# A two-layer graph network and an edge attention on one core: x scaled earlier, key rows turned in two parts, stores on another queue, and a rotated order of the attention

## The reference

```
h = relu(layernorm(x));  deg = max(edges into node, 1);  norm = deg ** -0.5
twice:   h = rrelu( segment_sum((rel[type] + h[src]) @ W_r, dst) * norm + where(no edge in, h @ W_el, h @ W_sl) )
x = x + h
h = relu(layernorm(x));  qk = h @ Wqk + bqk;  v = h @ Wv + bv
score(e) = clip(qk[dst] . qk[src] / sqrt(128), -5, 5);  a = softmax of score over the edges of one dst
out = segment_sum(a * v[src], dst) @ Wo + bo;  x = x + gamma * layernorm(out + h) + beta
```

## Time and profile before

| | us |
|---|---|
| median of three runs | 803.48 (803.4 to 803.63) |
| profiled execution | 803.2 |
| its span, first to last instruction | 800.6 |
| TensorE busy | 717.5 (90%) |
| VectorE busy | 515.5 (64%) |
| ScalarE busy | 431.3 (54%) |
| GpSimd busy | 258.0 (32%) |
| mean granted clock of TensorE | 0.984 |

### The profile page before, as it was taken

How to read it: one execution, slowest core, us unless ns; L and a number is a source line. 1 busy time by engine, 2 the same in 40 slices (tenths; PEclk the granted TensorE clock), 3 DMA queues, 4 the chain that set the end, 5 groups by cost and what they waited for, 6 DMA issues and landing times.

```text
span 800.6 us, 15393 instructions
## 1 busy us (share of the span) xinstructions
PE 717.5 (90%) x5767; PEld 533.3 (67%) x5767; DVE 515.5 (64%) x931; ACT 431.3 (54%) x1085; POOL 258.0 (32%) x273
## 2 busy tenths in 40 slices
PE   5268689897999999987999999799999999999995
PEld 3157588786889999876988999444444444444455
DVE  5999999986688877341333333434665757565667
ACT  0447866664466566652111111377676767677671
POOL 7140080000000222210000000256665766666663
PEclk9999999998999999989999999999999999999997
DMA  4101100133300000102222111210000000000000
GB/s 131 45 1 34 50 2 8 52 103 64 101 9 8 8 8 8 53 20 57 64 93 74 37 36 34 85 50 0 1 15 11 14 13 14 13 13 14 3 24 19
DMA packets 39763, 27.89 MB, mean 35 GB/s; under 512 B 5311, under 2 KB 38163, under 8 KB 39686
## 3 DMA queue, kind: packets, MB, share of 16 engines
q1 hardware_dynamic: 38356, 26.02, 11.2%
q10 hardware_dynamic: 1330, 0.86, 0.4%
HBM read 13.28 MB, written 10.80 MB: 30 GB/s over the span
## 4 chain that ended last, share of the span: by engine, by line
PE 65%; DVE 9%; DMA 8%; ACT 5%; issue 5%; SPq 5%; POOL 2%; ACTq 1%; POOLq 0%; DVEq 0%
PE sums L1467 16%; PE sums L1450 15%; PE sums L998 9%; PE sums L1071 9%; PE sums L1037 6%; DMA first_columns<-counts 2%; SPq L582 2%; DVE work L835 2%; DVE work L829 2%; SPq L572 2%; ACT counts L1243 2%; DMA h_layer_one<-work 1%; PE sums L1094 1%; PE sums L1005 1%; DMA h_attention<-work 1%
## 5 line engine op out<-in xcount | busy, mean ns | idle before, releaser
L1546 POOL TENSOR_TENSOR counts<-counts,work 125x500 f32<-125x500 f32 x150 | 165.6, 1104 | 96.7 <-DVE work L1607 89.6
L1037 PE MATMUL sums<-work 125*128 125x196 f16 (+15 forms) x1220 | 154.3, 253 | 22.3 <-DVE work L835 22.1
L1607 DVE SCALAR_TENSOR_TENSOR work<-sums,counts 125x500 f32<-125x500 f32 x150 | 101.7, 678 | 108.2 <-ACT sums L1564 108.2
L1467 PE MATMUL sums<-work 125*128 125x500 f32 (+1 forms) x350 | 159.0, 544 | 7.7 <-DVE work L1607 2.9
L1450 PE MATMUL sums<-work 128*125 128x500 f32 x300 | 150.3, 583 | 0.6 <-ACT work L1301 0.6
L1559 ACT ACTIVATE sums<-sums,work 125x500 f32<-125x500 f32 (+1 forms) x157 | 102.1, 650 | 76.3 <-PE sums L1450 73.1
L829 DVE TENSOR_TENSOR work<-work,counts 125x3024 f16<-125x3024 f16 (+1 forms) x60 | 114.2, 1903 | 36.9 <-PE sums L1039 33.7
L1243 ACT CAST counts<-sums 128x364 f32 (+38 forms) x305 | 131.8, 473 | 3.1 <-issue 1.1
L1039 PE MATMUL sums<-work 125*128 125x10 f16 (+15 forms) x800 | 131.6, 194 | 0.0
L835 DVE TENSOR_TENSOR work<-work,counts 125x4200 f16<-125x4200 f16 (+15 forms) x120 | 125.3, 1084 | 0.0
L998 PE MATMUL sums<-counts 125*128 125x250 f16 (+1 forms) x975 | 121.0, 269 | 3.4 <-ACT work L1181 3.2
(11 more groups left out here) (177 smaller groups left out, 686.5 us busy)
## 6 DMA issues: line engine op xcount, KB each, us to landing
first_columns<-counts SPq DMA_DIRECT2D x5, 610.4 KB
counts<-first_columns SPq DMA_DIRECT2D x5, 610.4 KB
counts<-counts SPq DMA_DIRECT2D x5, 468.8 KB
counts<-in_x SPq DMA_DIRECT2D x5, 312.5 KB
h_nodes<-counts SPq DMA_DIRECT2D x5, 312.5 KB
work<-in_x SPq DMA_DIRECT2D x12, 125.0 KB
x_after_messages<-work SPq DMA_DIRECT2D x12, 125.0 KB
h_attention<-work SPq DMA_DIRECT2D x12, 125.0 KB
```

The costliest lines, as they stand in the source:

```text
L1037: pe.matmul(win[:, 0:c, cols], lo[:, k * 2 * LO:k * 2 * LO + 128], m[:, k, h0 * w:(h0 + c) * w].rearrange("p (h d) -> p h d", d=w), start= ...
L1467: last = pe.matmul(ps_o[c % 2][:, 0:cols(u) // n], h3[:, j + i, :], pbuf[u % PB][:, i * NP:i * NP + cols(u) // n], start=j + i == 0, stop= ...
L1546: pool.tensor_tensor(a, a, p, ALU.add).then_inc(acc_done, 1)
L1607: dve.scalar_tensor_tensor(pbuf[u % PB], ps_s[u % 4][0:NP, 0:WIDE], float(np.exp(-CLIP)), counts[0:NP, j, c * WIDE:(c + 1) * WIDE], ALU.ma ...
```

## The change

- **Turning of keys.** TensorE turns only the first 12 of 100 rows of each key array before `first_keys`; the other rows follow once the four first copies are made, and ScalarE's later copies wait for them key by key.
- **Words.** VectorE packs `words` behind the ramp copy instead of ahead of `loc`.
- **Scaling of x.** SCALED goes from 34 to 16, ROUNDS and RESTS go forward with it; the statistics come behind batch 0, the checks behind batch 1, shift and flag behind batch 4 instead of 6, the parts of the relations behind batch 11 instead of 3. The addition of EPS goes from GpSimd to VectorE. FIRST_SLOT goes from 66 to 61.
- **Stores.** The stores of chunks 2 and 3 are issued from ScalarE's queue, at the groups `agg` + 2, which are 120 and 133.
- **Loads of layer two.** Wqk, bqk and the last rows of x are loaded from SP's queue, ahead of the first x; `weigh` waits for the three weights alone, and the first qk product and the last chunk wait for the three new ones.
- **Attention.** Target group c is (c + 1) mod 6, and source block j is (j + 4) mod 24, block 24 last, so it begins with targets 4 to 7 and source 4. Two of the first three scores are issued inside the last chunk of layer two, ahead of the turn of chunk 0. The six pieces of h3 are read in that order too, and only the fifth waits for the store of the last two chunks.

```diff
@@ -117,11 +117,12 @@
 READY = (58, 82, 100, 115, 128, 140, 151, 162, 171, 180, 189, 197, 200)
-FIRST_SLOT = 66
+FIRST_SLOT = 61
 KEY_TILES = 48
+FIRST_ROWS = KEY_TILES // RT
 MOVED = 44
@@ -339,9 +340,9 @@
-    SCALED = 34
-    ROUNDS = ((40, 45, 50, 55, 60), (48, 53, 58, 63, 68))
-    RESTS = ((12, 13, 14, 16, 17), (14, 15, 16, 18, 19))
+    SCALED = 16
+    ROUNDS = ((22, 27, 32, 37, 42), (30, 35, 40, 45, 50))
+    RESTS = ((7, 8, 10, 11, 12), (9, 10, 12, 13, 14))
@@ -576,11 +577,10 @@
                     sp.dma_start(counts[0:NP, i:i + 4, 3 * D + 48 * a:3 * D + 48 * a + 48], got[:, :, a, :]).then_inc(keys_moved, 16)
-            store(2)
             for i in range(5):
                 sp.dma_start(counts[0:NP, v, 0:3 * D], counts[0:NP, v, PART_AT:PART_AT + 3 * D]).then_inc(parts_moved, 16)
-            for c in range(3, DIRECT):
+            for c in range(4, DIRECT):
                 store(c)
@@ -602,6 +602,10 @@
             sp.wait_ge(y_done, CHUNKS)
+            sp.wait_ge(norm_set, CHUNKS)
+            sp.dma_start(wqk, wqk_d).then_inc(L["last_in"], 16)
+            sp.dma_start(bqk, bqk_d.rearrange("(p o) -> p o", o=1)).then_inc(L["last_in"], 16)
+            sp.dma_start(x_last, by_block(x, LAST)).then_inc(L["last_in"], 16)
             for i, c in enumerate(ORDER2[:-1]):
@@ -615,8 +619,10 @@
             sp.wait_ge(L["summed"], CHUNKS)
-            sp.wait_ge(L["h3_out"], 16 * LAST)
+            sp.wait_ge(L["h3_out"], 16 * (LAST - 2))
             for i, (j0, j1) in enumerate(T["h3_pieces"]):
+                if j0 == 0:
+                    sp.wait_ge(L["h3_out"], 16 * LAST)
                 if j0 == LAST * LB:
@@ -665,8 +671,7 @@
             pool.wait_ge(tables_done, 1)
-            pool.wait_ge(stats_done, NB)
-            link(pool.tensor_scalar(rstd, mv[:, :, 1], EPS, None, ALU.add))
+            pool.wait_ge(stats_done, 1)
             pool.tensor_tensor(rstd, rstd, power.broadcast_to([NP, NB]), ALU.pow).then_inc(root_x, 1)
@@ -713,13 +718,6 @@
             link(dve.tensor_tensor(by_tile(tb), by_tile(starts), over(gb), ALU.add))
-            dve.wait_ge(next_in, 16)
-            link(dve.tensor_copy(after[:, 0:1], gb[:, 1:2]))
-            link(dve.tensor_copy(after[:, 1:2], nxt_i))
-            link(dve.tensor_tensor(after, after, gb, ALU.subtract))
-            link(dve.tensor_tensor(after, after, room, ALU.min))
-            link(dve.tensor_scalar(after, after, 0.0, None, ALU.max))
-            dve.scalar_tensor_tensor(words, after, 4096.0, gb, ALU.mult, ALU.add).then_inc(words_done, 1)
             link(dve.tensor_tensor(tiles(loc), tiles(dst_i), tb[:, :, None].broadcast_to([ROWS, RT, NP]), ALU.subtract))
@@ -762,6 +760,13 @@
+            dve.wait_ge(next_in, 16)
+            link(dve.tensor_copy(after[:, 0:1], gb[:, 1:2]))
+            link(dve.tensor_copy(after[:, 1:2], nxt_i))
+            link(dve.tensor_tensor(after, after, gb, ALU.subtract))
+            link(dve.tensor_tensor(after, after, room, ALU.min))
+            link(dve.tensor_scalar(after, after, 0.0, None, ALU.max))
+            dve.scalar_tensor_tensor(words, after, 4096.0, gb, ALU.mult, ALU.add).then_inc(words_done, 1)
             for k in (0, 2):
@@ -773,7 +778,9 @@
                 for j in range(NB):
-                    dve.bn_aggr(mv[:, j, :], stat[:, j, :]).then_inc(stats_done, 1)
+                    last = dve.bn_aggr(mv[:, j, :], stat[:, j, :])
+                link(last)
+                dve.tensor_scalar(rstd, mv[:, :, 1], EPS, None, ALU.add).then_inc(stats_done, 1)
@@ -842,12 +849,12 @@
                 if b == 0:
+                    statistics()
+                if b == 1:
                     checks()
-                if b == 1:
-                    statistics()
-                if b == 3:
+                if b == 11:
                     relations()
-                if b == 6:
+                if b == 4:
                     dve.wait_ge(root_x, 1)
@@ -921,7 +928,7 @@
                 if i == LAST:
-                    dve.wait_ge(L["last_in"], 16)
+                    dve.wait_ge(L["last_in"], 16 * 3)
                 else:
@@ -953,13 +960,21 @@
             pe.wait_ge(consts, 2)
+
+            def turn(k, r0, r1):
+                out = key_ps[0:NP, k, :].rearrange("p (r t) -> p r t", t=RT)
+                for t in range(RT):
+                    last = pe.matmul(out[:, r0:r1, t], key16[k][:, t * NP:(t + 1) * NP], ident_h[0:ROWS, r0:r1], start=True, stop=True)
+                return last
+
             for k in range(4):
                 pe.wait_ge(nat_done, k + 1)
-                out = key_ps[0:NP, k, :].rearrange("p (r t) -> p r t", t=RT)
-                for t in range(RT):
-                    for r0, r1 in ((0, 64), (64, ROWS)):
-                        last = pe.matmul(out[:, r0:r1, t], key16[k][:, t * NP:(t + 1) * NP], ident_h[0:ROWS, r0:r1], start=True, stop=True)
+                last = turn(k, 0, FIRST_ROWS)
                 last.then_inc(keys_turned, 1)
+            pe.wait_ge(first_keys, 4)
+            for k in range(4):
+                turn(k, FIRST_ROWS, 64)
+                turn(k, 64, ROWS).then_inc(keys_turned, 1)
@@ -1086,7 +1101,7 @@
                 if i == 0:
-                    pe.wait_ge(L["wts"], 16 * 5)
+                    pe.wait_ge(L["wts"], 16 * 3)
                 pe.wait_ge(L["turned_out"], i + 1)
@@ -1101,6 +1116,8 @@
                 pe.wait_ge(L["h3_t_out"], i + 1)
+                if i == 0:
+                    pe.wait_ge(L["last_in"], 16 * 3)
                 pe.matmul(ps_q[:, 0:w], wqk, h3_t[:, 0:w], start=True, stop=True).then_inc(L["qk"], 1)
@@ -1134,14 +1151,16 @@
                     pe.wait_ge(L["ident"], 2)
+                if i == LAST:
+                    pe.wait_ge(L["rows"], 3)
+                    A["tensor_first"](pe, 0, 2)
                 if i:
-            pe.wait_ge(L["rows"], LAST)
-            A["tensor_first"](pe)
+            A["tensor_first"](pe, 2, 3)
@@ -1160,8 +1179,8 @@
                 act.copy(*key_copy(k, 0)).then_inc(first_keys, 1)
-            act.wait_ge(first_keys, 4)
             for k in range(4):
+                act.wait_ge(keys_turned, 5 + k)
                 for piece in (1, 2, 3):
@@ -1207,9 +1226,15 @@
+
+            act_stores = {at_slot["agg", c] + 2: c for c in (2, 3)}
             act.wait_ge(words_in, 16)
             for g in range(GROUPS):
+                if g in act_stores:
+                    c = act_stores[g]
+                    act.wait_ge(y_done, c + 1)
+                    act.dma_start(h1_dram[:, c * LB * D:(c + 1) * LB * D], t1.rearrange("p b f -> p (b f)")).then_inc(h1_out, 16)
                 if g % CHUNK == 0:
@@ -1286,9 +1311,6 @@
                 act.dma_start(t, v).then_inc(L["wts"], 16)
-            act.dma_start(wqk, wqk_d).then_inc(L["wts"], 16)
-            act.dma_start(bqk, bqk_d.rearrange("(p o) -> p o", o=1)).then_inc(L["wts"], 16)
-            act.dma_start(x_last, by_block(x, LAST)).then_inc(L["last_in"], 16)
@@ -1396,6 +1418,9 @@
+    target = lambda c: (c + 1) % FULL if c < FULL else FULL
+    source = lambda c, j: (j + AB) % (FULL * AB) if c < FULL and j < FULL * AB else j
+
     units = [(c, j, 1) for c in range(FULL) for j in range(NB)] + [(FULL, j, min(AB, NB - j)) for j in range(0, NB, AB)]
@@ -1420,7 +1445,7 @@
     def rows(v, c, h, n):
-        at = c * WIDE + 2 * h * NP
+        at = target(c) * WIDE + 2 * h * NP
         return v[at:at + n * NP, :].rearrange("(b p) f -> p b f", p=NP)
@@ -1443,18 +1468,18 @@
         c, j, n = units[u]
-        if u == NB - 1:
-            pe.wait_ge(T["rows"], -(-NB // 2))
+        if u in (FULL * AB - AB, NB - 1):
+            pe.wait_ge(T["rows"], -(-NB // 2) - (u < NB - 1))
         out = ps_s[u % 4]
         if c < FULL:
-            last = pe.matmul(out[0:NP, :WIDE], qk_t[:, j * NP:(j + 1) * NP], qk_t[:, c * WIDE:(c + 1) * WIDE], start=True, stop=True)
+            last = pe.matmul(out[0:NP, :WIDE], qk_t[:, source(c, j) * NP:(source(c, j) + 1) * NP], qk_t[:, target(c) * WIDE:(target(c) + 1) * WIDE], start=True, stop=True)
         else:
-    def tensor_first(pe):
-        for u in range(AHEAD):
+    def tensor_first(pe, u0, u1):
+        for u in range(u0, u1):
             score(pe, u)
@@ -1464,7 +1489,7 @@
             for i in range(n):
-                last = pe.matmul(ps_o[c % 2][:, 0:cols(u) // n], h3[:, j + i, :], pbuf[u % PB][:, i * NP:i * NP + cols(u) // n],
+                last = pe.matmul(ps_o[c % 2][:, 0:cols(u) // n], h3[:, source(c, j + i), :], pbuf[u % PB][:, i * NP:i * NP + cols(u) // n],
                                  start=j + i == 0, stop=j + i == NB - 1)
@@ -1495,7 +1520,7 @@
                 for s, (j0, _) in zip(T["h3_in"], T["h3_pieces"]):
-                    if j == j0:
+                    if source(c, j) == j0:
                         pe.wait_ge(s, 16)
@@ -1604,7 +1629,7 @@
         if c < FULL:
```

(6 more changed lines are left out.)

## The result

| | us |
|---|---|
| before, median of 22 runs | 804.15 (801.61 to 808.76) |
| changed, median of 22 runs | 800.89 (794.65 to 808.24) |
| ratio, 95% interval | 0.9956 [0.9939, 0.9973] |
| profiled execution after | 801.75, span 800.0 |

A forecast was written before the change was run, and what follows sets the result against it. VectorE bounds 20 to 150 us, then TensorE, with waits along SP's queue to about 345. Terms +1.65 - 6.8 - 2.7 - 1.5 = -9.35 from 803.2 gave 793.85, plus 0.28: 794.1 us; 8-in-10 range 789.5 to 799.5.

The forecast's parts named there:

- The start: Kernel start: words packed later hold ScalarE's key copies, so VectorE's first batch starts 1.45 us later; EPS adds 0.2.
- Scaling from group 16: Earlier scaling of x, about even: +1.5 us of waits against -1.5 us of VectorE's waits for TensorE taken back.
- waits for h_nodes: Early chain: VectorE's moved rests come up to half a microsecond late on the h_nodes stores, +1.5 us (0 to 5).
- all of it back: Early chain: the 1.45 us that VectorE idles for TensorE is recovered whole, -1.5 us (0 to -1.5).
- The middle: Counting: stores 2 and 3 on ScalarE's queue remove the h_layer_one wait, -6.8 us (-9 to -2).
- three place loads: Middle: ScalarE's loads at groups 132, 136, 140 fall into SP's parts moves, charged 1.2 us each, 3.6 in all.
- rival D: Middle: ScalarE's store issue at group 133 is held until SP's parts moves are issued; slower, 807 us; chance 0.07.
- Rival B: Start not held and slow place loads miss the parts moves: -2.3 and -2, 790 us; chance 0.18.
- Rival C: Middle: the gain is mostly given back, each place load costing 2.3 us, 798 us; chance 0.10.
- Layer two: First weighing waits for three loads instead of five, TensorE goes on at about 374.8: -2.7 us (0 to -3.0).
- Into the attention: Layer two's end: scores ahead of the last turn and earlier h3 pieces start the first weighted sum sooner, -1.5 us.
- Rival A: Early chain costs 6 us instead of 1.65, through ScalarE's pace and the landing of h_nodes: 798.5 us; chance 0.15.

The follow-up runs named there:

- experiment 9: Changed kernel with its whole early part put back as before; stores, layer-two loads and attention order kept: ratio 0.9873 to the kernel before, 792.97 us.
- Experiments 1 to 3: On the changed kernel: statistics back behind batch 1, 0.9955; words packed ahead of loc again, 0.9981; both edits, 0.9893 (ratios to the kernel before).
- Experiment 1: Changed kernel with the statistics back behind batch 1 and the checks behind batch 0: ratio 0.9955 to the kernel before.
- experiment 5: Kernel before with only the stores of chunks 2 and 3 issued by ScalarE: ratio 0.989, 795.58 us.
- experiment 7: Changed kernel with its three added loads issued on ScalarE's queue behind the weights: ratio 0.9962 to the kernel before.
- Experiments 12: Experiment 9's kernel with the first load of the heads held until the three weights have landed: ratio 0.9864 to the kernel before, 791.41 us.

## Why the prediction was wrong

- **The step that failed: "The start" and "Scaling from group 16", summed to +1.65 us; measured +7.5 at group 107, and +6.7 in the ratios (experiment 9 against the changed kernel).** The mechanism, that a late VectorE passes all of it on, was right. Its terms, forecast and measured: the start +1.45 and +1.3; waits for h_nodes +1.5 and +2.05; VectorE's waits for TensorE -1.5 and +0.7 (2.70 in all, before 1.95); waiting for x, 0 and +2.8; the rest, all of it busy time, +0.2 and +0.6.
- The missing term was x. I wrote that batch 0, the statistics and batch 1 "need only first_keys". That is false of the statistics: the kernel has them wait for all five loads of x. I had asked of the moved step what it covers, not what it needs. Its input was in no row that I read: the statistics before began at 31.6 us with no wait, so the trace gave only an upper end for the landing. From the place that the statistics got (24.9: 22.1 and the length of batch 0) to 31.6 that end is 6.7 us, and with it in the range 794.1 would have reached to 800.8. Experiments 1 to 3 show the term: taken away alone (2.1 us at group 107), hidden behind it the gain of the words (nothing), and with both gone 6.8 us.
- The waits for TensorE did not go: taking "all of it back" at the far end of its range, with no row for it, was a choice for the favourable end. The 1.45 us were also no measure of these waits: they are the idle time of two of the stages between 20 and 150 us, while the waits up to group 107 were 1.95 us. Experiment 1 showed that time saved ahead of that wait is partly spent in it.
- **The middle was right in its mechanism**, the wait for the store, and near in size, partly by luck: -6.3 for -6.8, and alone -7.5 (experiment 5). Of the three place loads one was long enough to matter. Rivals C (given back) and D (held on ScalarE) fell; rival D lives from a hold of some 11 us, and the store's issue took 0.50 us in the middle of SP's moves at 3.75 each. Rival B fell with VectorE's first batch at 22.03, behind 2.31 us of waiting for ScalarE's copies. Rival C's 798 is also not what its own terms give: three loads at 2.3 instead of 1.2 us are 3.3 more, 797.4.
- **Layer two was mis-sized**: -2.7 forecast for the weights, -1.2 measured (8.53 to 7.29 us). In the medians nothing of it can be told: experiments 5 and 9 differ by 1.4 us (0.989 to 0.9873), and the attention's order alone gave 1.5. The landing of 3.6 us in the earlier trace rows did not hold once W_el was waited for (5.8), so the wait turned from bqk to W_el; most likely it never was the landing of W_el (experiment 7). In the profile, slower products behind the wait then cost 1.6 us, more than the 1.2 gained; experiment 9 has nearly the same wait (2.15 us) and products at full speed behind it, so the wait alone does not bring that loss.
- **Into the attention was right**: -1.8 for -1.5, kept to the end.
- Rival A ("the early chain costs more", 6 us, 798.5) comes nearest to the result and had 0.15. It named the landing of h_nodes and ScalarE's pace; x was the larger part. One of my signs of being wrong came, narrowly: VectorE waited 2.05 us on h_nodes, and the limit was 2.

## What to carry to other kernels

When a step is moved forward, look up the landing of every tile that it reads, and where the trace shows no wait, charge the move with the time between its new place and its old. A wait on the engine that is the wall can have a second one close behind it, as here: words and statistics brought nothing each alone and 0.6% together (0.9956 to 0.9893), and moving the rests uncovered ScalarE's loads. A landing shown for one load of a semaphore that several raise may be the time of the count and not of that load: here W_el read 3.6 us with five loads on its semaphore and 5.8 with three, in the same order on the same queue (experiment 7).

## What the runs showed of the hardware

In these runs the granted clock of a stretch did not by itself say how long its products took. From 60 to 90 us it was 1.00 in the profile of the kernel before and 0.50 in that of the changed one, and the commonest product of the counting took 292 and 291 ns (busy us, then mean ns of one):

```profile
L1037 PE MATMUL sums<-work 125*128 125x125 f16 x64 | 11.3, 292 | 2.7 <-DVE work L835 2.7
```
```profile
L1052 PE MATMUL sums<-work 125*128 125x125 f16 x64 | 11.8, 291 | 0.0
```

Experiments 12 (0.50) and 9 (1.00) have the very same program up to there:

```profile
60.00:90.00 30.00, 23.56 (x269) 20.36 (x266) 29.44 (x26) 24.17 (x84) 0.00 (x0) 0.50 0.14 38
```
```profile
60.00:90.00 30.00, 23.57 (x269) 20.45 (x267) 29.45 (x26) 24.08 (x84) 0.00 (x0) 1.00 0.14 37
```

TensorE is busy for as long with as many products, and group 107 stands at 153.70 and 153.76 us. Nor do whole runs of the changed kernel differ by it: of the 20 runs in the ratio, 9 had a mean granted clock of 0.92 to 0.94 and a median of 801.0 us, 11 one of 0.98 and above and 800.8 us. The changed kernel's 0.50 is therefore not what made its early part slow. At most it had a share in the wait of 1.09 us at 108 us: from 90 to 103 us products of 175 columns took 333 ns each in the changed kernel and 288 before.

Elsewhere the clock shows in the time, and not in large products alone. From 376 to 380 us, behind the wait for the weights, the four f32 products of 256 columns took 1.96 us in the changed kernel (granted clock 0.66 from 375 to 380 us) and 1.13 in the kernel before and in experiment 9 (1.00), and six f16 products of 125 columns 311 ns each for 218 before. Why it does not show from 60 to 90 us stays open.

In the changed kernel two queues issued side by side: ScalarE's issue of a store took 0.50 us beside SP's moves at 3.75 each (18.75 for five), while ScalarE's small load of four places (L1240), 0.93 us at the median of 14 from 140 to 226 us, took 4.51 us there at the longest. In this kernel it is the load, not the issue, that must be kept away from such moves.
